# A causal convolution by 128-row filter blocks: nine block products instead of ten, in the first three of four row blocks

## The reference

```python
xn = layernorm(x)                                  # 2048 rows of 512
K  = s4_kernel(Lambda, p, q, Vc @ Bp, Ct, exp(log_step))   # a filter of 512 numbers
s  = irfft(rfft(xn, 1024) * rfft(K, 1024))[..., :512] + D * xn   # causal convolution
h1, h3 = lora_linear(xn, w1, A1, B1), lora_linear(xn, w3, A3, B3)   # 512 -> 1376
g  = silu(lora_linear(silu(h1) * h3, w2, A2, B2))  # 1376 -> 512
out = x + s * g
```

## Time and profile before

| | us |
|---|---|
| median of three runs | 428.47 (427.99 to 428.89) |
| the profiled execution | 428.78 |
| its span, first to last instruction | 427.0 |
| TensorE busy | 419.1 (98%) |
| VectorE busy | 161.1 (38%) |
| ScalarE busy | 102.6 (24%) |
| GpSimd busy | 65.5 (15%) |

### The profile page before, as it was taken

The page is one execution under the profiler, slowest core; times in us unless marked ns, Lnnn a source line. Parts: engine busy times, 40 slices in busy tenths (PEclk is TensorE's granted clock), DMA queues, the critical chain, the costliest instruction groups (busy, mean ns, idle before and its releaser), DMA issues.

```text
span 427.0 us, 5022 instructions
## 1 busy us (share of the span) xinstructions
PE 419.1 (98%) x1868; PEld 341.2 (80%) x1868; DVE 161.1 (38%) x245; ACT 102.6 (24%) x168; POOL 65.5 (15%) x128
## 2 busy tenths in 40 slices
PE   8999999999999999999999999999999999999995
PEld 7977888887778888888788888888778888888773
DVE  4658586655486221224135222132324111111115
ACT  5543323333232111122112111212212111111111
POOL 3246725332050103200000101400000000000000
PEclk9999999999999999999999999999999999999999
DMA  8474822321315301000004301000002000000002
GB/s 266 118 222 128 310 81 73 89 81 31 97 66 178 118 2 50 2 0 0 2 22 149 124 0 50 0 0 0 0 0 99 0 0 0 0 0 0 0 0 98
DMA packets 14064, 26.19 MB, mean 61 GB/s; under 512 B 2481, under 2 KB 4209, under 8 KB 14033
## 3 DMA queue, kind: packets, MB, share of 16 engines
q1 hardware_dynamic: 13888, 25.41, 18.9%
q0 software_dynamic: 160, 0.59, 0.4%
HBM read 20.37 MB, written 4.53 MB: 58 GB/s over the span
## 4 chain that ended last, share of the span: by engine, by line
PE 95%; DVE 2%; DMA 1%; issue 1%; ACT 0%; SPq 0%; DVEq 0%; ACTq 0%
PE h L782 20%; PE h L783 20%; PE h L784 20%; PE f L784 9%; PE f L782 9%; PE f L783 9%; PE spare L769 2%; DMA lora_first<-lora_dram 1%; DVE w L625 1%; PE spare L764 1%; PE f L777 1%; PE spare L784 1%; PE spare L782 1%; PE spare L783 1%; DVE raw L615 0%
## 5 line engine op out<-in xcount | busy, mean ns | idle before, releaser
L782 PE MATMUL h<-xt,w 128*128 (+4 forms) x356 | 138.7, 390 | 0.2 <-DVE w L625 0.2
L784 PE MATMUL h<-xt,w 128*128 (+4 forms) x356 | 137.8, 387 | 0.0
L783 PE MATMUL h<-xt,w 128*128 (+4 forms) x356 | 137.8, 387 | 0.0
L782 PEld LDWEIGHTS h<-xt,w 128*128 128x128 f32 (+1 forms) x356 | 66.0, 185 | 15.9 <-DVE w L625 0.6
L784 PEld LDWEIGHTS h<-xt,w 128*128 128x128 f32 (+1 forms) x356 | 66.0, 185 | 14.9
L661 DVE TENSOR_TENSOR g<-g,h 128x512 f32<-128x512 f32 (+1 forms) x44 | 30.2, 687 | 126.1 <-PE h L784 126.1
L783 PEld LDWEIGHTS h<-xt,w 128*128 128x128 f32 (+1 forms) x356 | 66.0, 185 | 14.5
L666 DVE TENSOR_TENSOR ghl<-g,ghl 128x512 fp32r<-128x512 f32 (+1 forms) x44 | 32.0, 727 | 101.1 <-ACT ghl L521 101.0
L784 PE MATMUL f<-ghl,w2f 128*128 128x512 f32 (+1 forms) x176 | 69.5, 395 | 0.0
L782 PE MATMUL f<-ghl,w2f 128*128 128x512 f32 (+1 forms) x176 | 69.4, 395 | 0.0
L783 PE MATMUL f<-ghl,w2f 128*128 128x512 f32 (+1 forms) x176 | 69.2, 393 | 0.0
(11 more groups left out here) (103 smaller groups left out, 274.8 us busy)
## 6 DMA issues: line engine op xcount, KB each, us to landing
raw<-w_dram SPq DMA_DIRECT2D x28, 256.0 KB, 3.7
xres<-xT_dram SPq DMA_DIRECT2D x4, 1024.0 KB, 6.9
outT_dram<-xres SPq DMA_DIRECT2D x16, 256.0 KB, 2.4
rows_next<-x_dram SPq DMA_DIRECT2D x4, 512.0 KB, 3.7
scale_rows<-scales_scratch SPq DMA_DIRECT2D x3, 512.0 KB, 4.1
xn<-x_dram SPq DMA_DIRECT2D x4, 256.0 KB, 4.2
rows<-x_dram SPq DMA_DIRECT2D x2, 512.0 KB, 7.4
raw<-w_dram SPq DMA_DIRECT2D x4, 224.0 KB, 2.5
```

Of the source, the lines that this page charges most:

```text
L782: pe.matmul(out, w[1], m[0], start=start, stop=False)
L783: pe.matmul(out, w[0], m[1], start=False, stop=False)
L784: return pe.matmul(out, w[0], m[0], start=False, stop=stop)
```

## The change

In blocks 0, 1 and 2 the convolution is made of nine block products. The middle products T1 x1 and T0 x0 are made first, one in each spare bank. ScalarE copies T1 x1 into g (`middle_copy`). Output 0 is T0 x0. Output 2 gets T2 x0 and T0 x2 in bank h1, and VectorE adds g. Output 3 is made as before, in h3. Output 1 is the product of T0 + T1 with x0 + x1 (`convolve_sums`, into the spare bank that held T1 x1), less g, to which VectorE has added T0 x0. The sum T0 + T1 is made once and x0 + x1 once for each block, by GpSimd (`add_rows`), and both are split into high and low parts with ScalarE's help (`sum_hi`). The outputs' order becomes 2, 3, 0, 1. Block 3 keeps ten products and the old order, and on TensorE and VectorE it has code of its own for that. ScalarE's first Silu of a block waits for `m_taken`, since g is in use until VectorE has subtracted it.

```diff
-        conv = [sp[0], sp[1], h3, h1]
-        OUT_ORDER = (3, 2, 1, 0)
+        conv = [sp[0], sp[1], h1, h3]
+        OUT_ORDER, LAST_ORDER = (2, 3, 0, 1), (3, 2, 1, 0)
...
@@ ScalarE
+                if j == 0 and (not isinstance(b, int) or b > 0):
+                    act.wait_ge(m_taken, b)
                 nc.scalar.activation(g[0:hs(j), :], h1[0:hs(j), :], ACT.Silu).then_inc(silu_done, 1)
...
+            def sum_hi(b):
+                act.wait_ge(x_sum_ready, b + 1)
+                nc.scalar.copy(x_sum[0][:, :], x_raw[1][:, :]).then_inc(x_sum_hi, 1)
+
+            def middle_copy(b):
+                act.wait_ge(m_ready, b * 2 + 1)
+                act.wait_ge(glo_done, b * HT + HT)
+                nc.scalar.copy(g[:, :], conv[1][:, :]).then_inc(m_copied, 1)
...
+                            act.wait_ge(t_sum_ready, 1)
+                            nc.scalar.copy(t_sum[0][:, :], t_raw[:, :]).then_inc(t_sum_hi, 1)
+                        if not first and not last and (j, place) == (1, "down"):
+                            sum_hi(b)
+                if not last:
+                    middle_copy(b)
                 for c in () if last else norm_at["out"]:
                     next_hi(b + 1, c, par_next)
-                out_gate(b)
+                if first:
+                    sum_hi(b)
+                out_gate(b, LAST_ORDER if last else OUT_ORDER)
...
@@ VectorE, out_sum
+                    if c == 0:
+                        dve.wait_ge(m_copied, b + 1)
+                        dve.wait_ge(m_ready, b * 2 + 2)
+                        nc.vector.tensor_tensor(g[:, :], g[:, :], conv[0][:, :], ALU.add).then_inc(m_added, 1)
+                    if c == 2:
+                        dve.wait_ge(m_copied, b + 1)
+                        dve.wait_ge(conv_ready, b * CONVS + CONV_NO[c] + 1)
+                        nc.vector.tensor_tensor(conv[2][:, :], conv[2][:, :], g[:, :], ALU.add).then_inc(c2_whole, 1)
+                        dve.wait_ge(c2_whole, b + 1)
                     dve.wait_ge(gate_done, e + 1)
-                    dve.wait_ge(conv_ready, e + 1)
+                    if c == 1:
+                        dve.wait_ge(m_added, b + 1)
+                        nc.vector.tensor_tensor(g[:, :], g[:, :], gate[:, n % 2, :], ALU.mult).then_inc(m_gated, 1)
+                        dve.wait_ge(m_gated, b + 1)
+                        wait_residual(dve, b)
+                        nc.vector.tensor_tensor(resid(par, c), resid(par, c), g[:, :], ALU.subtract).then_inc(m_taken, 1)
+                        dve.wait_ge(m_taken, b + 1)
+                    if c != 0:
+                        dve.wait_ge(conv_ready, b * CONVS + CONV_NO[c] + 1)
...
@@ TensorE
+            def convolve_sums(b):
+                pe.wait_ge(m_copied, b + 1)
+                pe.wait_ge(x_sum_lo, b + 1)
+                three(conv[1][:, :], [t_sum[hl][:, :] for hl in (0, 1)], [x_sum[hl][:, :] for hl in (0, 1)], True, True) \
+                    .then_inc(conv_ready, 1)
...
+                middle_products(b, par, first)
+                down_wait(b, HT - 1)
+                down_chunk(HT - 1, 2).then_inc(f_ready, 1)
+                convolve_2(b, par)
+                down_chunk(HT - 1, 3).then_inc(f_ready, 1)
+                convolve_3(b, par)
+                down_chunk(HT - 1, 0).then_inc(f_ready, 1)
+                down_chunk(HT - 1, 1).then_inc(f_ready, 1)
+                convolve_sums(b)
...
@@ GpSimd
+            def add_rows(b, par):
+                pool.wait_ge(xlo_done, b * DC + DC)
+                tt(x_raw[0][:, :], xt[:, par, 0, 0, :].bitcast(F32), xt[:, par, 0, 1, :].bitcast(F32), ALU.add) \
+                    .then_inc(x_sum_step, 1)
+                tt(x_raw[1][:, :], xt[:, par, 1, 0, :].bitcast(F32), xt[:, par, 1, 1, :].bitcast(F32), ALU.add) \
+                    .then_inc(x_sum_step, 1)
+                pool.wait_ge(x_sum_step, b * 2 + 2)
+                tt(x_raw[1][:, :], x_raw[0][:, :], x_raw[1][:, :], ALU.add) \
+                    .then_inc(x_sum_ready, 1)
+                pool.wait_ge(x_sum_hi, b + 1)
+                tt(x_sum[1][:, :], x_raw[1][:, :], x_sum[0][:, :].bitcast(F32), ALU.subtract) \
+                    .then_inc(x_sum_lo, 1)
+                pool.wait_ge(x_sum_lo, b + 1)
...
             next_scale(1, 1)
+            pool.wait_ge(tz_lo, 1)
+            add_rows(0, 0)
             with pool.Fori(1, NBLK - 1) as b:
+                pool.wait_ge(conv_ready, b * CONVS)
+                add_rows(b, b % 2)
                 for r in range(0, RT, 2):
                     rows_rstd(b + 1, r)
-                pool.wait_ge(conv_ready, b * DC)
                 next_scale(b + 1, (b + 1) % 2)
```

More of the change, by code:

```diff
@@ L227, in build @@
         ghl = put("ghl", [P, 2, BLK], F32R)
+        tz_off = top[0]
         tz = put("tz", [P, D])
         tzs = put("tzs", [P, 2, D], F32R)
+        eye_off = top[0] + EYE * 4
         lane_c = put("lane_c", [P, EYE + P])
@@ L329, in build @@
         s4_step = sem("s4_step")
+        x_sum_step, x_sum_ready, x_sum_hi, x_sum_lo = map(sem, ("x_sum_step", "x_sum_ready", "x_sum_hi_done", "x_sum_lo_done"))
+        t_sum_ready, t_sum_hi, t_sum_lo = map(sem, ("t_sum_ready", "t_sum_hi_done", "t_sum_lo_done"))
+        m_ready, m_copied, m_added, m_gated, m_taken, c2_whole = map(sem, ("m_ready", "m_copied", "m_added", "m_gated", "m_taken", "c2_whole"))
         def w13_tile(kind, j, hl):
@@ L425, in store @@
             def store(b, par):
-                for n, c in enumerate(OUT_ORDER):
+                for n, c in enumerate(LAST_ORDER if isinstance(b, int) and b == NBLK - 1 else OUT_ORDER):
                     sync.wait_ge(res_done, b * DC + n + 1)
@@ L718, in body @@
                         next_lo(b + 1, c, par_next)
-                out_sum(b, par)
+                if last:
+                    last_sum(b, par)
+                else:
+                    out_sum(b, par)
             nc.vector.memset(g[:, 0:P], 0.0).then_inc(g_cleared, 1)
@@ L855, in down, with block_times, middle_products, convolve_2 @@
                 mm.then_inc(g_used, 1)
-            def convolve(b, par, c_out, first):
-                t = b * HT + HT
+            def block_times(out, b, par, k, c, start, stop):
+                return three(out[:, :], [tzs[:, hl, k * P:(k + 1) * P] for hl in (0, 1)],
+                             [xt[:, par, hl, c, :] for hl in (0, 1)], start, stop)
+            def middle_products(b, par, first):
+                for c in (1, 0):
+                    out = take(b, ("conv", b, c), first)
+                    block_times(out, b, par, c, c, True, True).then_inc(m_ready, 1)
+            def convolve_2(b, par):
+                pe.wait_ge(silu_done, b * HT + HT)
+                block_times(conv[2], b, par, 2, 0, True, False)
+                block_times(conv[2], b, par, 0, 2, False, True).then_inc(conv_ready, 1)
+            def convolve_3(b, par):
+                pe.wait_ge(g_done, b * HT + HT)
+                for c in range(DC):
+                    mm = block_times(conv[3], b, par, DC - 1 - c, c, c == 0, c == DC - 1)
+                mm.then_inc(conv_ready, 1)
+            def convolve_sums(b):
[3 more added lines that the diff above has]
+                    .then_inc(conv_ready, 1)
+            def convolve(b, par, c_out):
                 if c_out < 2:
-                    out = take(b, ("conv", b, c_out), first)
+                    out = take(b, ("conv", b, c_out), False)
                 else:
-                    pe.wait_ge((g_done, silu_done)[c_out - 2], t)
+                    pe.wait_ge((silu_done, g_done)[c_out - 2], b * HT + HT)
                     out = conv[c_out]
                 for c in range(c_out + 1):
-                    k = (c_out - c) * P
-                    mm = three(out[:, :], [tzs[:, hl, k:k + P] for hl in (0, 1)],
-                               [xt[:, par, hl, c, :] for hl in (0, 1)], c == 0, c == c_out)
+                    mm = block_times(out, b, par, c_out - c, c, c == 0, c == c_out)
                 mm.then_inc(conv_ready, 1)
@@ L890, in extras, with body @@
                     mm.then_inc(krow_ready, 1)
-            def body(b, par, first):
+            def body(b, par, first, last):
                 if first:
@@ L922, in body @@
                     pe.wait_ge(tz_lo, 1)
+                    pe.wait_ge(t_sum_lo, 1)
                     wait_split(pe, 2, HT - 1)
[L925 to L936, removed]
+                if last:
+                    for n, c in enumerate(LAST_ORDER):
+                        if n < DC - 1:
+                            convolve(b, par, c)
+                        if n == 0:
+                            down_wait(b, HT - 1)
+                        down_chunk(HT - 1, c).then_inc(f_ready, 1)
+                        if n == DC - 1:
+                            convolve(b, par, c)
+                    return
+                middle_products(b, par, first)
+                down_wait(b, HT - 1)
```

(11 more changed lines are left out.)

25 lines of the change are left out of this document (22 added, 3 removed).

## The result

The changed kernel takes 435.14 us (median of four, 434.98 to 435.31), the kernel before, timed beside it, 428.68. The ratio is 1.0152 with a 95% interval of 1.0134 to 1.017: slower by 6.5 us, where 435.2 was predicted. Nine matmuls are gone (1859 instead of 1868), and the span grew from 427.0 to 433.3 us; the chain that ended last is TensorE for 90% instead of 95%.

A forecast was written before the change was run, and what follows sets the result against it. TensorE was taken to bound the kernel (95% of the last chain). Block changes +6.6, +0.6, -0.35 and small edits -0.2 gave +6.7: span 433.7, profiled 435.4, median level 435.2 us; 80% range 431.8 to 438.2.

The forecast's parts named there:

- The saving: TensorE, blocks 0 to 2: three matmuls fewer per block at 0.232 us, 0.70 per block, 2.1 us in all.
- Wait 1: Block ends: TensorE waits for the last hidden tile's low part, 0.87 us in block 0, 0.35 in blocks 1 and 2.
- Wait 2: Block 0: convolve_sums waits for x_sum_lo from a relay over GpSimd and ScalarE; TensorE idle 4.7 us, block 1 +4.6.
- The turn-taking: Block 0: GpSimd and VectorE instructions with two SBUF inputs alternate, one pair costing about 1.75 us.
- Wait 3: Next block's first Silu waits for m_taken: +2.05 us in block 0 to 1, +0.95 in 1 to 2, then nothing.
- rival B: Block 0's 4.7 us idleness lowers TensorE's clock behind it: 0 to +4 us, say +2.5, giving 437.7; 13%.
- Smaller edits: Filter sum hidden, perhaps sparing the wait at 103.6 (-0.2 us); block 3's old order and loading the next rows cost 0.
- A: GpSimd and VectorE hardly block each other in the new places: +1.1 us, 429.6; 10%.
- C: Faster: waits 2 and 3 find cover, leaving 1.4 us of the nine matmuls' saving: 427.1; 3%.
- D: The change costs what it saves, the total staying within 0.2%; 2%.
- B's reading of rows 10: At the kernel's start, 256-column matmuls 0.21 apart, later 0.12, were read as a clock step from 1.2 to 2.4 GHz.

The follow-up runs named there:

- five: four, with VectorE making outputs 0 and 1 only after the next block's tile 0, and statistics, shifts and low parts one tile later: 425.94 us.
- conv2_first: The changed kernel with output 2's two products ahead of the wait for the last hidden tile, instead of behind it: 434.45 us.
- late_rows: The changed kernel with GpSimd starting add_rows in the loop only when tile 0's low part is made: 433.56 us.
- own_tile: The changed kernel with the middle product T1 x1 copied to a tile of its own instead of g: 433.72 us.
- keep_up: The changed kernel with 17 idle matmuls in block 0's gap before convolve_sums: 436.27 us.
- keep_up_own: The changed kernel with the edits of keep_up and own_tile together: 432.8 us.
- changed_2: The changed kernel run again without an edit, on the same chip as keep_up_2: 435.06 us.
- early_rows: The changed kernel with GpSimd's add_rows in block 0 ahead of next_scale, and ScalarE's rounding after tile 10's Silu: 431.28 us.
- four: early_rows, own_tile and conv2_first together, plus VectorE making output 2's addition and product ahead of the last three low parts in block 0: 428.58 us.
- after: The changed kernel itself, in its first profile; timed median 435.14 us.
- keep_up_2: keep_up run again without an edit, beside changed_2: 436.08 us.

## Why the prediction was right, point by point

**The saving.** With all waits gone, five gets 0.65 in block 0 to 1, 0.68 in block 1 to 2 and 0.68 in block 2 to the end, against 0.70 predicted for each.

**Wait 1.** Predicted stalls of 0.87 and 0.35; the changed kernel shows 0.85 in block 0 (inside the second wait, by conv2_first) and 0.37 in each of the others.

**Wait 2.** From the first convolution matmul of block 0 to the resumed one the sum had 132.0 - 118.04 = 13.96; measured are 131.08 - 117.50 = 13.58. The turn-taking was right in order and nearly in size: adds of 1.74, 1.74 and 1.61, shifts of 3.46 for two. One step differs: GpSimd's last subtraction runs beside VectorE's low parts (1.68) and starts earlier, instead of alone behind them (1.25). The turn-taking is shown by late_rows as well, which removes it at another place.

**Wait 3.** Block 1 to 2: predicted +0.6, measured +0.92; its stall was 1.1 to 1.25 (what own_tile and late_rows gain) instead of 0.95. In block 0 to 1 the prediction had 4.6 + 2.05 = 6.6 and the trace gives 6.48, but the parts are not as the prediction put them. The 2.05 was to be idle time before the 25th matmul. What filled it was half-rate matmuls, and the idle time left there is below 0.1 us. The forecast and rival B both occurred in one place. The prediction's own sign for B, and for being wrong, was matmuls 0.45 apart behind the gap; they stand 0.43 apart. So on this point it was wrong: its forecast left the clock at the full level. B was given 13% and a likely price of +2.5; the clock fell in all five profiles that have the gap, and the price in the first was zero, the lower end given for it ("of which m_taken's 2.05 is there anyway: 0 to +4"). own_tile, keep_up and keep_up_own show how the two lie: each alone taken away gives 0.18 and 0.02, both together 1.75. That the price was zero is luck in part: the eleven slow matmuls lost about 2.2 us, and the Silu's wait alone is 2.0 in keep_up. In late_rows the slow stretch lost 2.7.

**Smaller edits.** -0.2 was predicted, and block 0's convolution begins 0.54 earlier in the profiled execution; the executions' beginnings also differ (changed_2 has 118.37), so this term is not settled. The written-out block 3 costs nothing that shows: from the first convolution matmul of block 2 to that of block 3, 97.55 against 97.84 before, where -0.35 was predicted, and from there to the last matmul 9.51 against 9.52.

**Rivals.** A (hardly any blocking) is refuted by the durations and by late_rows. C and D needed cover that was not there. B's reading of rows 10 as a step of the clock has no support in the granted clock of that trace, which reads 1.00 from 13.4 to 13.8; it has some from early_rows, where the same 256-column matmuls stand 0.21 apart at a granted clock of 0.50.

**The arithmetic.** 433.7 and 1.78 make 435.48, not 435.4. A range for two terms each off by half would be 431.9 to 438.5 if both went one way; 432.8 to 437.3 is narrower, and the prediction doesn't say why.

In all, the three waits, their causes and their sizes were right, and the total was right with them. The clock was wrong, and it did not show in the total because its loss fell beside wait 3.

## What to carry to other kernels

A product saved on the bounding engine is worth its start-to-start distance, and here 0.7 us a block was less than either wait that its new inputs brought (4.2 us for the sum of the rows, 1.1 to 2.0 for m_taken); each new input should be made while its engine is idle, not where its loop happens to stand (early_rows: 3.9 us in block 0 for moving GpSimd's four instructions and ScalarE's rounding). Two delays that end at the same instruction do not add up, so removing one of them can show nothing, and it takes the run with both removed to see either. When a wait goes, look for the next instruction behind the same engine's queue: four moved a wait by 36 matmuls and gained nothing, five took VectorE's late outputs out from ahead of it.

## What the runs showed of the hardware

TensorE's granted clock fell to half in all five profiles that have the gap of 4.2 to 5.1 us before convolve_sums (after, own_tile, conv2_first, late_rows, changed_2): in four of them while TensorE still stood idle, in changed_2 about when it started again. Behind the gap 8 to 13 matmuls then stood 0.43 apart instead of 0.23, which lost 1.6 to 2.7 us. In keep_up_2 it fell 1.6 us after the end of a wait of 1.84 us, in the midst of back-to-back matmuls, so the cost can arrive after the work has resumed. The same wait in keep_up's first profile, and the waits of 1.6 us in early_rows and 1.9 us in four, show no fall, so it does not come each time.

GpSimd's 128x512 addition took 1.29 us beside VectorE's products with one PSUM input, and these kept 0.68 beside it:

```profile
133.15 1.29 POOL L1062 TENSOR_TENSOR x_sum_a<-xt 128x512 f32 x1 [2.22 <-PE spare L852]
133.71 0.68 DVE L739 TENSOR_TENSOR gate<-gate,spare 128x512 f32<-128x512 f32 x1
```

Beside VectorE instructions with two SBUF inputs it took 1.74, and these took 1.77 instead of 0.69. The Trainium skill, "SBUF — State Buffer", Who interferes with whom, says that a VectorE instruction with two SBUF inputs contends with a GpSimd instruction that reads SBUF, and that one with at most one SBUF input does not; the traces agree with both.
